# Cross-attention and a gated low-rank layer on one core: steps of two quarters ordered by tile shape

## What is computed

```python
def _L0_xattn_ref(q, k, v):                      # all (8, 512, 2048); 8 heads of 64 channels
    qh = softmax(q as (B, N, H, dh), axis=3)     # over the 64 channels of a head
    kh = softmax(k as (B, N, H, dh), axis=1)     # over the 2048 positions
    kvs = jnp.einsum('bnhd,bnhe->bhde', kh, vh)
    return jnp.einsum('bnhd,bhde->bnhe', qh, kvs)   # turned back to (B, C, N)

def _L0_ffn_ref(x, router_w, A, B):
    logits = flat @ router_w.T                   # 4 experts
    gates = softmax of the two largest logits, the others 0
    mid = jnp.einsum('tf,erf->ter', flat, A)     # rank 16
    all_deltas = jnp.einsum('ter,eor->teo', mid, B) * 4
    return jnp.einsum('te,teo->to', gates, all_deltas)

x = x + _L0_xattn_ref(_layernorm(x), ctx, ctx)
x = x + _L0_ffn_ref(_layernorm(x), router_w, A, B)
```

## Time and profile before

| | before |
|---|---|
| median of 3 runs | 455.8 us (454.64 to 456.86) |
| the profiled execution's own time | 454.94 us |
| its span | 453.2 us |
| TensorE matmul busy | 422.5 us (93%) |
| VectorE busy | 379.1 us (84%) |
| ScalarE busy | 311.0 us (69%) |
| GpSimd busy | 358.9 us (79%) |
| granted TensorE clock, mean | 0.969 |
| moved by DMA | 137.59 MB, mean 304 GB/s |

### The profile page before, as it was taken

How to read it: one execution, slowest core, us unless ns; L and a number is a source line. 1 busy time by engine, 2 the same in 40 slices (tenths; PEclk the granted TensorE clock), 3 DMA queues, 4 the chain that set the end, 5 groups by cost and what they waited for, 6 DMA issues and landing times.

```text
span 453.2 us, 16801 instructions
## 1 busy us (share of the span) xinstructions
PE 422.5 (93%) x6888; PEld 382.3 (84%) x6888; DVE 379.1 (84%) x1045; ACT 311.0 (69%) x436; POOL 358.9 (79%) x343
## 2 busy tenths in 40 slices
PE   6558998999999999999999999999999999999975
PEld 6557887898989898998989898998989898999864
DVE  3468777898998989898998989898989989775864
ACT  1265979695968778695958777785959777775310
POOL 0466999999898989898898989898988988994610
PEclk9667999999999999999999999999999999999988
DMA  8995888779999999999999999999999998454247
GB/s 286 420 409 188 307 290 271 248 276 321 364 297 372 339 340 344 307 341 332 351 310 361 331 346 341 307 352 333 357 316 338 310 366 269 173 186 187 95 185 279
DMA packets 38972, 137.59 MB, mean 304 GB/s; under 512 B 4208, under 2 KB 6384, under 8 KB 38768
## 3 DMA queue, kind: packets, MB, share of 16 engines
q1 hardware_dynamic: 38896, 136.52, 86.5%
HBM read 102.95 MB, written 33.55 MB: 301 GB/s over the span
## 4 chain that ended last, share of the span: by engine, by line
PE 71%; DVE 10%; POOL 6%; DMA 4%; issue 3%; SPq 3%; ACT 1%; POOLq 0%; DVEq 0%; ACTq 0%
PE num_ps L407 21%; PE kv_ps L390 14%; PE raw_ps L423 11%; PE delta_ps L471 10%; PE kv_ps L438 6%; PE delta_ps L472 6%; DMA ctx_sb<-in_ctxt_dram 4%; DVE y_sb L709 3%; POOL y_sb L323 3%; POOL ek_sb L311 3%; DVE attnT L700 2%; DVE bn_parts L642 2%; DVE midT L800 1%; PE raw_ps L457 1%; SPq L235 1%
## 5 line engine op out<-in xcount | busy, mean ns | idle before, releaser
L311 POOL TENSOR_TENSOR ek_sb<-ctx_sb,kmax_row 128x512 f32<-128x512 f32 x128 | 167.8, 1313 | 36.5 <-ACT kmax_row L504 36.5
L323 POOL TENSOR_TENSOR y_sb<-attnT,y_sb 128x512 f32<-128x512 f32 x128 | 164.3, 1284 | 31.0 <-DVE attnT L700 31.0
L407 PE MATMUL num_ps<-kv_sb,x_sb 128*128 128x130 f32 x1024 | 141.1, 281 | 9.0 <-DVE attnT L700 6.0
L407 PEld LDWEIGHTS num_ps<-kv_sb,x_sb 128*128 128x128 f32 x1024 | 126.0, 192 | 12.9 <-issue 8.7
L709 DVE TENSOR_TENSOR y_sb<-delta_ps,y_sb 128x512 f32<-128x512 f32 x128 | 87.3, 684 | 23.7 <-PE delta_ps L472 22.8
L625 DVE TENSOR_REDUCE max_n<-ctx_sb 128x32 f32<-128x512 f32 x128 | 86.5, 677 | 10.8 <-DMA ctx_sb<-in_ctxt_dram 10.8
L390 PE MATMUL kv_ps<-ctx_sb,ek_sb 128*64 128x65 f32 x2048 | 92.8, 233 | 0.3 <-ACT ek_sb L526 0.3
L700 DVE TENSOR_TENSOR attnT<-num_ps,rden 128x512 f32<-128x512 f32 x128 | 88.5, 691 | 4.8 <-DVE rden L697 0.4
L390 PEld LDWEIGHTS kv_ps<-ctx_sb,ek_sb 128*64 128x64 f32 x2048 | 74.2, 139 | 17.8 <-issue 5.8
L526 ACT ACTIVATE ek_sb<-ek_sb 128x1024 f32<-128x1024 f32 x64 | 67.1, 1049 | 26.9 <-POOL ek_sb L311 26.9
L423 PE MATMUL raw_ps<-w_sb,y_sb 128*64 128x69 f32 x2048 | 84.5, 223 | 0.0
(11 more groups left out here) (63 smaller groups left out, 398.3 us busy)
## 6 DMA issues: line engine op xcount, KB each, us to landing
ctx_sb<-in_ctxt_dram SPq DMA_DIRECT2D x64, 520.0 KB, 5.3
x_sb<-in_x_dram SPq DMA_DIRECT2D x64, 512.0 KB, 6.1
y_sb<-in_xt_dram SPq DMA_DIRECT2D x64, 512.0 KB, 6.3
out_dram<-y_sb SPq DMA_DIRECT2D x60, 512.0 KB, 6.2
out_dram<-y_sb SPq DMA_DIRECT2D x8, 256.0 KB, 3.6
sq_a<-in_bt_dram SPq DMA_DIRECT2D x1, 1024.0 KB, 15.8
w_sb<-in_wt_dram SPq DMA_DIRECT2D x1, 552.0 KB, 9.6
cst<-in_consts_dram SPq DMA_DIRECT2D x1, 145.0 KB, 2.3
```

Source lines behind the costliest of these rows:

```text
L311: pool.tensor_tensor(ek_sb[:, t % 2, chunks(g), :].rearrange("p (a b) c -> p a b c", b=2), ctx_sb[:, t % 4, 2 * g:2 * g + 2, 1:P + 1, :].r ...
L323: pool.tensor_tensor(y, attnT[:, g, :], y, ALU.add).then_inc(x1_made, 1)
L407: mm = pe.matmul(num_ps[:, j // 2, at:at + 2 * (DH + 1)], x_sb[:, t % 4, c * P:(c + 1) * P], kv_sb[:, t % 2, :], start=True, stop=True, sk ...
```

## The change

All loops go through q two quarters at a time, from -10 to 148 (`range(FIRST, LAST + 1, 2)`), and the calls in a step stand in a new order. TensorE's order goes by the shape of the weights: numerators of the first quarter, two deltas, numerators of the second quarter, then both quarters' kv, then both quarters' projection. Offsets move by a quarter or two (numerators from 5 to 6, projection from 7 to 8, deltas from 21 to 22).

* delta_ps is one buffer of two banks; VectorE adds both with one instruction per step, 64 instead of 128. `max_part` takes 64 channels at once, 64 calls instead of 128. The turned maxima go to a corner of delta_ps; deltas wait until they have been read.
* Tiles whose number is not a multiple of 4 have their first statistics on ScalarE, the others on VectorE (`on_act`).
* GpSimd adds x for the first quarter of a step in it, and for the second one in the step after. The gates' selection comes last in a step on VectorE, and their sum, reciprocal, scale and product go to the step after it.
* At the start w is summed over chunks by VectorE (`fold_weights`) and over partitions by one matmul; w is loaded behind the third context tile, B last and into the space of y_sb's slot 7, b_hi is made at q = 10 and b_lo at 14 and 18.
* The last pair is stored with four DMAs instead of eight.

The core of the diff:

```diff
-    FIRST = -8
-    LAST = 4 * (NT - 1) + 29
+    FIRST = -10
+    LAST = 4 * NT + 20
...
-        b_rows = sq_a[:].rearrange("p h n -> p (h n)")
+        b_rows = y_sb[:, 7, :, :].rearrange("p j c -> p (j c)")
...
-        delta_ps = [bank("delta_ps0"), bank("delta_ps1")]
-        max_ps = num_ps[:, 0, 3 * P:4 * P]
+        delta_ps = bank("delta_ps", (P, 2, 512))
+        max_ps = delta_ps[:, 0, 0:P]
...
+        def on_act(t):
+
+            return t % 4 != 0
...
             def store_last(i):
-                c = slice(2 * i, 2 * i + 2)
+                c = slice(4 * i, 4 * i + 4)
...
-            sp.dma_start(w_sb[:], wt).then_inc(w_landed, 16)
             whole(load_x, 1)
             whole(load_ctx, 2)
+            sp.dma_start(w_sb[:], wt).then_inc(w_landed, 16)
             whole(load_y, 0)
-            sp.dma_start(b_rows, bt).then_inc(b_landed, 16)
-            whole(load_y, 1)
             whole(load_x, 2)
             whole(load_ctx, 3)
+            whole(load_y, 1)
+            sp.dma_start(b_rows, bt).then_inc(b_landed, 16)
...
-                    after(sp, raw_done, quarters_done(q, 7))
+                    after(sp, raw_done, quarters_done(q, 8))
...
-            for q in range(FIRST, LAST + 1):
-                root1(q)
-                shift(*tile_at(q, -3))
-                root2(q)
-                add_x(*tile_at(q, 5))
+            for q in range(FIRST, LAST + 1, 2):
+                add_x(*tile_at(q - 1, 6))
+                root2(pair_in(q, 18))
+                shift(*tile_at(q, -2))
+                add_x(*tile_at(q, 6))
+                shift(*tile_at(q + 1, -2))
+                root1(tile_in(q, 2))
...
-                after(pe, attn_made, 4 * (t - 3) + 3)
+                after(pe, out_made, adds_until(4 * t - 4))
...
-                    pe.wait_ge(kmax_made, min(t + 3, NT))
...
-                after(pe, out_made, 8 * p + i - 1)
+                if i % 2 == 0:
+                    after(pe, out_made, 4 * p + i // 2)
+                    after(pe, kmax_made, min((8 * p + i + 22) // 4 + 2, NT))
...
             def sum_w():
-                pe.wait_ge(w_landed, 16)
-                for j in range(NCH):
-                    mm = pe.matmul(raw_ps[1][:, 0, 0:NQ], ones, w_sb[:, j, :], start=(j == 0), stop=(j == NCH - 1))
-                mm.then_inc(w_summed, 1)
+                pe.wait_ge(w_folded, 1)
+                pe.matmul(raw_ps[1][:, 0, 0:ER + E], ones, w_fold[:], start=True, stop=True).then_inc(w_summed, 1)
...
-            for q in range(FIRST, LAST + 1):
+            for q in range(FIRST, LAST + 1, 2):
+                turn_max(tile_in(q, -4))
+                numerator(*tile_at(q, 6))
                 delta(*delta_at(q))
-                turn_max(q)
-                sum_squares(q)
-                if q == 1:
+                delta(*delta_at(q + 1))
+                sum_squares(tile_in(q, 12))
+                if q == 4:
                     sum_w()
-                numerator(*tile_at(q, 5))
-                spread_kmax(q)
-                kv(*tile_at(q, 0))
-                project(*tile_at(q, 7))
-                fold_squares(q)
-                turn_mid(q)
+                spread_kmax(tile_in(q, -4))
+                numerator(*tile_at(q + 1, 6))
+                turn_mid(pair_in(q, 20))
+                for k in range(2):
+                    kv(*tile_at(q + k, 0))
+                for k in range(2):
+                    project(*tile_at(q + k, 8))
+                fold_squares(tile_in(q, 10))
...
+            for q in range(FIRST, LAST + 1, 2):
+                T = q // 4
+                if q % 4 == 0:
+                    copy_squares(T - 3)
+                    copy_kv(T - 1)
+                    keys(T, 0)
+                    spread_row(T + 1)
                     square_x1(T - 2, 0)
-                    copy_kv(T - 1)
+                    queries(T - 1, 0)
+                    mid_high(pair_in(q, 20))
                     sum_x(T + 1)
-                if r == 1:
+                else:
                     keys(T, 1)
-                    spread_row(T + 1)
                     square_x1(T - 2, 1)
+                    gate_exp(pair_in(q, 18))
                     queries(T - 1, 1)
-                if r == 2:
-                    gate_exp(q)
                     square_x(T + 1)
-                if r == 3:
-                    copy_squares(T - 2)
-                    keys(T + 1, 0)
-                    queries(T, 0)
...
-                if q == 0:
+                if q == 10:
                     act.wait_ge(b_landed, 16)
                     act.activation(b_hi[:], b_rows, ACT.Copy).then_inc(b_hi_made, 1)
...
-                dve.wait_ge(delta_done, 8 * p + i + 1)
-                y = y_sb[:, pair_slots(p), 2 * i:2 * i + 2, :]
-                dve.tensor_tensor(y, delta_ps[i % 2][:].rearrange("p (j t c) -> p t j c", j=2, t=2), y,
+                dve.wait_ge(delta_done, 8 * p + i + 2)
+                y = y_sb[:, pair_slots(p), 2 * i:2 * i + 4, :]
+                dve.tensor_tensor(y, delta_ps[:].rearrange("p b (j t c) -> p t (b j) c", j=2, t=2), y,
                                   ALU.add).then_inc(out_made, 1)
...
+            def fold_weights():
+                dve.wait_ge(w_landed, 16)
+                dve.tensor_reduce(w_fold[:], w_sb[:, :, 0:ER + E].rearrange("p j n -> p n j"), AX.X,
+                                  ALU.add).then_inc(w_folded, 1)
```

240 lines of the change are left out of this document (124 added, 116 removed).

## The result

The changed kernel took 449.85 us (median of 6 executions, 449.35 to 453.67), the kernel before 456.61 (454.64 to 457.43) on the same chip: a ratio of 0.9877 (of the means) with a 95% interval of 0.9852 to 0.9901. That is 1.2% faster, 6.8 us by the medians, where 14.2 us and 3.2% were forecast. The sign was right, 449.85 lies in the range of 431 to 453, and the forecast time was missed by 8.9 us.

The account below looks back on a forecast made before the run. The prediction took TensorE's own work to bound the middle, with VectorE, GpSimd and ScalarE close below. Middle -9.0, start -6.8 and end +1.6 summed to -14.2 us, so 441 us, range 431 to 453.

Parts of the forecast that it names:

- The entries: Middle: TensorE pays 0.17 entering half-width tile shape and 0.20 entering full width; four of eight 0.37 leave a pair.
- The full step's lateness: Middle, step with gates, mid and first statistics: VectorE 0.65 us late, TensorE waits, 0.33 a pair.
- The hand-off: Middle: second numerators wait for VectorE's normalising, 2.27 start to restart; with small gate operations 0.82 us a pair.
- a doubled VectorE operation: Middle: one VectorE instruction replacing two 512-element ones costs between 0.69 and 1.20 us; 1.15 taken.
- rival 3: Middle: ScalarE becomes the bound of tiles with statistics, 8.8 us, giving 449.5; chance 0.12.
- rival 4: Middle: fewer waits than counted, a pair at 24.0, 16.1 us less, giving 434; chance 0.12.
- Rival 1: Middle: handed-off numerators late at most steps because of VectorE's fixed order, 20.8 us, giving 461; chance 0.10.
- Tile 2's first numerators start at 18.2 + 31.3 = 49.5: Start: maxima row made at 18.2, then 31.3 us of ScalarE work; tile 2 at 49.5 against 56.42 before.
- the b_lo operations, now in the running steps, cost 1.0: Start, tile 2 to tile 4: b_lo adds 1.0 to 23.0, putting tile 4's first numerators at 73.5.
- The gains for fewer steps and for the store: End: four steps fewer, about 1.0 less to the last normalising; last store and queueing 1.2 less.
- The rounds: End: four rounds of TensorE's last-pair deltas and VectorE's addition, 3.2 us each, 12.8 in all, 4.9 more.
- the hand-offs ahead of the last pair's deltas: End: hand-offs 1.1 us less, with fewer adds in front of the gates.

Follow-up runs that it names:

- the split projection: Changed kernel with the first of a step's two projections moved back before the second numerators, so TensorE changes tile shape two more times a step: 461.86 us.
- b_lo in VectorE's gap: Changed kernel with VectorE's prologue work (weights, b_lo) moved to where VectorE waits for the second numerators in early steps: 442.43 us.
- the fillers' kernel: Changed kernel with 16 unread transposes on TensorE in each of steps 8, 16 and 20, where it would idle: 445.73 us.

## Why the prediction was right in sign and wrong in size

**The middle was right in its mechanism and overpriced one term.** 24.20 a pair against 24.55. The entries were sized 0.17 and 0.20; the split projection measured 0.16 and 0.19. The full step's lateness, 0.65, measured 0.67. The hand-off was to take 2.27 from start to restart plus 0.38 a pair for gate operations between reciprocal and product; it took 2.12 and 2.19, and the gate operations cost nothing. That term alone is 0.38, and the difference is 0.35. Other terms were off by little: TensorE restarted 0.06 behind the product instead of 0.14 (258.87 + 0.69 to 259.62), and a doubled VectorE operation took 1.21 to 1.23 where 1.15 was taken. TensorE was busy 308.50 of 314.63 us, 23.7 of 24.2 a pair, where I had said 23.4 of 24.5. A wait of 0.2 hardly shows there, since the modelled end of the last delta's record (0.28) reaches past the 0.12 after which its like start. The only waits listed for TensorE between 100 and 400 us are those for attnT, so rival 3 (ScalarE as the bound, 449.5) has the measured total by a mechanism that did not occur; rival 4 (24.0 a pair) had the middle nearly right, but not the total. Rival 1 is refuted with it: VectorE was late once in four tiles, not at most steps.

**The start failed, in two steps of the sum.** The first numerators came at 27.83, near the 26.5. Then, first, "Tile 2's first numerators start at 18.2 + 31.3 = 49.5". The row came at 18.22, and ScalarE's 31.3 us of work was right, but I put it end to end, with no wait in it. In the profile ScalarE then waited 0.80, 0.87, 2.29 and 1.39 us, 5.35 in all, and tile 2's numerators came at 55.45, 5.95 late. The 2.29 stands behind the centring of the weights, which the sum never priced. Second, "the b_lo operations, now in the running steps, cost 1.0". From tile 2 to tile 4 the changed kernel took 32.0 us in its slowest execution, the forecast's 24.0 and 8.0 more, and 25.67 in its fastest, 1.7 more. With b_lo in VectorE's gap the same stretch took 23.95 (52.36 to 76.31), so the 23.0 + 1.0 held once nothing stood ahead of the kv reciprocals. I had costed the prologue's operations by their length alone, and by neither what was queued behind them on VectorE nor what GpSimd did beside them. In the profile ScalarE's copy of kv ends TensorE's idling, as one of my tests for "wrong" had it, but the copy was itself waiting for VectorE's reciprocals.

**The clock was in the sum for the end only.** Behind an idle time of 2.3 us it fell in one execution and not in the other (4.70 against 3.18 for the step), and the step from 81.22 to 87.45 took 6.23 at a clock of 0.50, where the fillers' kernel took 3.33 at 1.00. The forecast gave the start no term for it, though the kernel before showed 0.95 in its filling stretch and 0.77 ahead of it.

**The end was undersized.** +4.7 against +1.6. The two profiles, counted from tile 30's first numerators, divide it:

| | before | forecast | after |
|---|---|---|---|
| to the end of the last normalising | 21.57 | 1.0 less | 20.73 |
| from there to the last pair's first delta (before: to 440.90) | 11.27 | 1.1 less | 12.32 |
| from there to the end of the last addition | 7.85 | 4.9 more | 13.51 |
| from there to the end of the span | 4.45 | 1.2 less | 3.26 |

The gains for fewer steps and for the store came. The rounds took 3.39 instead of 3.2, 0.8 of the miss. The term that failed is the hand-offs ahead of the last pair's deltas: 1.1 less was booked, and it became 1.05 more. In the profile after, the low half of midT, which those deltas need, stands behind an addition of both banks on VectorE:

```profile
433.39 1.22 DVE L724 TENSOR_TENSOR y_sb<-delta_ps,y_sb 128x1024 f32<-128x1024 f32 x1 [0.38 <-PE delta_ps L488]
434.64 0.43 DVE L824 TENSOR_TENSOR midT<-raw_ps,midT 64x256 fp32r<-64x256 f32 x1
```

ScalarE's high half had ended at 434.19, so this is some 0.4 of the 1.05; in the kernel before the shorter addition was over (439.81) before the high half was (440.38). The rest of the 1.05 was not tried.

**Together, in medians.** The miss of 8.9 is the start's, plus 3.1 of the end, less 13 x 0.35 = 4.6 of the middle, so the start's is 10.4. That puts tile 4's numerators at 83.9 in a median execution, an estimate, which lies between the 79.22 and 87.45 of the two profiles. With the prologue in the gap the median falls by 7.5, which makes 76.4, and the profile has 76.31. The remaining 2.8 were lost before tile 2 (52.36 instead of 49.5). My own test, "tile 4's numerators come after 78", failed in both profiles. That the total lies in the range of 431 to 453 is partly luck, since the middle's surplus of 4.6 covered a part of what the start and the end lost.

## What to carry to other kernels

Price a one-off operation by the chain that stands behind it on its engine, and by what the neighbour engine does beside it: 1.3 us of VectorE work ahead of a reciprocal cost more than 2 us of TensorE, and in a gap where the engine waits anyway it cost nothing. Order TensorE's work by tile shape where one entry can serve two groups, and look for the wait that the missing cover opens. Where TensorE idles for 2 us, compare the next step with the same step at full clock, and do not price anything by one profile: here two of one kernel differ by 8.2 us up to tile 4.

## What the runs showed that I had not expected

**VectorE and GpSimd wait for each other when VectorE reads two SBUF operands.** Centring the weights took 2.36 us beside GpSimd's addition at 33.86 (1.28 us) in the changed kernel. With the prologue in the gap it started first, and it was the other way round. From that profile, VectorE and then GpSimd:

```profile
36.96 1.28 DVE L754 TENSOR_TENSOR w_sb<-w_sb,w_mean 128x1088 f32<-128x1088 f32 x1
```

```profile
37.12 2.27 POOL L343 TENSOR_TENSOR y_sb<-attnT,y_sb 128x512 f32<-128x512 f32 x1 [0.85 <-DVE attnT L715]
```

1.28 became 2.36 on one engine or 2.27 on the other: the later one waits for about what is left of the earlier. Likewise one b_lo took 0.68 us where it started first (GpSimd's addition beside it then took 1.66), and up to 1.81 in the changed kernel. The product attnT, which reads num_ps in PSUM, took 0.69 in the mean of 128. The kernel before showed it already, in its own b_lo. Beside GpSimd's operations from 26.92 to 31.62 one took 1.62, and the first behind them 0.68:

```profile
27.15 1.62 DVE L843 TENSOR_TENSOR b_lo<-sq_a,b_hi 128x512 fp32r<-128x512 f32 x1
31.64 0.68 DVE L843 TENSOR_TENSOR b_lo<-sq_a,b_hi 128x512 fp32r<-128x512 f32 x1
```

The Trainium skill (GPSIMD Engine Reference, Specifications) says that GpSimd shares its SBUF interfaces with VectorE and contends with VectorE instructions that have two SBUF inputs; the rows agree. By the rows, b_lo and the centring would have been priced at twice their length. It also makes the start uneven: whether b_lo of q = 18 meets GpSimd's addition (3.39 us) or not (1.39) differs between two executions of the same kernel.

**Work of no use made the kernel faster**, by 4.2 us for 48 transposes, and its executions more even. And the clock did not follow from the idling alone: behind 2.3 us of it, the same step ran at a mean clock of 0.64 in one execution and 1.00 in another.
